# A routed feed-forward layer in row tiles of 128 instead of 256, two inner blocks per round, rows transposed two tiles ahead

## The chip, the core and the metric

The kernel is one program on one core of a Trainium2 chip. The metric is the device time of one execution, in microseconds (us); a measurement is the median of several executions. TensorE (PE) multiplies, and loads the stationary operand of a matmul by an instruction of its own (LDWEIGHTS, shown as PEld); VectorE (DVE) and ScalarE (ACT) work on elements, GpSimd (POOL) and SyncE (SP) here issue DMA transfers. Every engine runs its own instruction stream, in order. Streams are held together by semaphores: an engine raises one with an instruction (`then_inc`), another waits for it (`wait_ge`).

## The reference

A block of two attention layers and two routed feed-forward layers on 4 x 512 tokens of width 256, float32. The change touches the last layer alone. It has 8 experts in 4 groups of 2; each token goes to one group (the largest sigmoid score), and within it both experts are used with normalised weights:

```python
macro_scores = jax.nn.sigmoid(xf @ macro_w)
mv, mi = _topk_normalized(macro_scores, GROUPS_TOP_K)        # one group of four
micro_scores = jax.nn.sigmoid(jnp.einsum('td,gde->tge', xf, micro_w))
uv, ui = _topk_normalized(micro_scores, TOP_K)               # both experts of a group
...
gate = jax.nn.silu(jnp.einsum('td,edf->tef', xf, gate_w))    # inner width 512
up = jnp.einsum('td,edf->tef', xf, up_w)
h = gate * up
out = jnp.einsum('te,tef,efd->td', w, h, down_w)
```

The result is added to the residual stream.

## The kernel before

`build` runs seven phases one after the other; each ends with all engines done. The last two are `phase_route1` and `phase_experts1`. The first normalises the rows, picks each token's group, and scatters the rows (256 values, two weights and the token's number) into the scratch array `sorted`, ordered by group. Each group's rows begin at a multiple of TILE, so that every tile of TILE rows belongs to one group. With TILE = 256 there are 2048/256 + 3 = 11 tiles, 2816 rows with the padding; the table `tile_group` says which group a tile belongs to. All tiles are worked, padded rows too.

`phase_experts1` works tile by tile. Its weights, `experts1`, lie in SBUF as two half-precision parts, hi and lo, and so do the activations; each product is three matmuls (`three_products`, lines 197 to 199: hi by hi, lo with hi, hi with lo). Call such a group of three matmuls a triple. A tile has two parts in TensorE's program:

- `head`: four 128x128 transposes of the tile's rows into `h_tb` (line 1766); then the first layer, 8 blocks of the inner width (2 experts x 4) of 4 triples each (gate and up, two halves of the 256-wide input). The weights are the stationary operand, the turned rows the moving one, 256 columns wide. A block fills one of two `h_hb` buffers.
- `tail`: the second layer, for each half of 128 rows 8 triples into `h_ob`, with the inner activations stationary and 256 columns of `down` moving: 16 triples.

That is 96 + 48 matmuls a tile, all with 256 columns moving, and 1584 in all.

Around it, ACT copies the turned rows to half precision (`xt.hi`, line 1700) and DVE forms the rest (`xt.lo`, line 1720). For each block ACT applies silu (line 1705), DVE multiplies (`h`, line 1725), ACT and DVE split the product into `hs` (lines 1710, 1728). After the second layer DVE weighs and adds the two experts (`first`, `res`, lines 1734 and 1739), and POOL scatters the result with an accumulating indirect DMA (line 1691, one for each 128 rows), always after the scatters of the tile before have landed. SP loads tiles (line 1674).

`run_tiles` gives PE, ACT and DVE the same order: head 0, then head j+1 before tail j; two tiles make one turn of a loop (`Fori`). On PE the wait that a first layer begins with is for the `xt.lo` of its own tile, right behind its transposes (line 1768). A block waits until the `h_hb` that it overwrites has been read by DVE (line 1771).

Which group a tile has is known only at run time. `expert_base` (line 1753) therefore loads a register from `tile_group`, and every address in `experts1` is computed from it by register instructions in PE's own stream.

Of the kernel before, what the change touches and what calls it, by code (L numbers as in the profile page):

```python
# [8 lines left out]
ALU = mybir.AluOpType  # L9
ACT = mybir.ActivationFunctionType  # L10
# [6 lines left out]
P = 128  # L17
# [1618 lines left out]
def phase_experts1(nc, sem, T, dram, out):  # L1636

    with ExitStack() as ctx:
        sb, ps = make_tensors(nc, ctx)
        rows = [sb(f"h_rows{i}", [P, 2, ROW]) for i in range(2)]  # L1640
        weight = [sb(f"h_weight{i}", [P, 2, PER_GROUP + 1]) for i in range(2)]
        token = [sb(f"h_token{i}", [P, 2], I32) for i in range(2)]
        xt = [Split(sb, f"h_xt{i}", [P, DT, TILE]) for i in range(2)]
        silu = [sb(f"h_silu{i}", [P, TILE]) for i in range(2)]
        h = [sb(f"h_h{i}", [P, TILE]) for i in range(2)]
        HT = PER_GROUP * FT1
        hs = [Split(sb, f"h_hs{i}", [P, HT, TILE]) for i in range(2)]
        first = [sb(f"h_first{i}", [P, 2, D]) for i in range(2)]
        res = [sb(f"h_res{i}", [P, 2, D]) for i in range(2)]
        tb = [ps(f"h_tb{i}", [P, DT, TILE]) for i in range(2)]  # L1650
        hb = [ps(f"h_hb{i}", [P, 2, TILE]) for i in range(2)]
        ob = [[ps(f"h_ob{i}_{n}", [P, PER_GROUP, D]) for n in range(2)] for i in range(2)]
        names = ("rows_in0", "rows_in1", "turned", "xt_hi", "rows_free", "xt_lo", "h_full", "silu_ok", "h_ok", "h_hi", "h_lo", "out_done",
                 "first_ok", "res_ok", "res_free", "stored")
        (rows_in0, rows_in1, turned, xt_hi, rows_free, xt_lo, h_full, silu_ok, h_ok, h_hi, h_lo, out_done,
         first_ok, res_ok, res_free, stored) = (sem("h" + n) for n in names)
        rows_in = (rows_in0, rows_in1)

        def run_tiles(eng, head, tail):

            head(0, 0)
            with eng.Fori(0, TILES1 // 2) as m:
                head(m * 2 + 1, 1)
                tail(m * 2, 0)
                head(m * 2 + 2, 0)
                tail(m * 2 + 1, 1)
            tail(TILES1 - 1, 0)

        with nc.Block() as block:

            @block.sync
            def _(sp):
                def load(j):
                    sp.dma_start(rows[j % 2][:], dram["sorted"][j * TILE:(j + 1) * TILE, :].rearrange("(n p) d -> p n d", p=P)).then_inc(rows_in[j % 2], 16)

                load(0)
                load(1)
                for j in range(2, TILES1):
                    sp.wait_ge(rows_free, j - 1)
                    load(j)  # L1680

            @block.gpsimd
            def _(pool):
                pool.sem_inc(res_free, 2)
                for j in range(TILES1):
                    pool.wait_ge(res_ok, j + 3)
                    if j >= 1:
                        pool.wait_ge(stored, 32 * j)
                        pool.sem_inc(res_free, 1)
                    for n in range(2):  # L1690
                        pool.indirect_dma_start(out=out, out_offset=bass.IndirectOffsetOnAxis(ap=token[j % 2][:, n:n + 1], axis=0),  # L1691
                                                in_=res[j % 2][:, n, :], in_offset=None, bounds_check=B * S - 1, oob_is_err=False,
                                                compute_op=ALU.add).then_inc(stored, 16)
                pool.wait_ge(stored, 32 * TILES1)

            @block.scalar
            def _(act):
                def head(j, i):
                    act.wait_ge(turned, j + 1)
                    nc.scalar.activation(xt[i].hi[:], tb[i][:], ACT.Copy).then_inc(xt_hi, 1)  # L1700
                    for g in range(HT + 1):
                        if g < HT:
                            act.wait_ge(h_full, j * HT + (g + 1))
                            act.wait_ge(h_ok, j * HT + (g + 1))
                            nc.scalar.activation(silu[g % 2][:], hb[g % 2][:, 0, :], ACT.Silu).then_inc(silu_ok, 1)
                        if g >= 1:
                            act.wait_ge(h_ok, j * HT + (g + 2))
                            if g == 1:
                                act.wait_ge(out_done, j + 1)
                            nc.scalar.activation(hs[i].hi[:, g - 1, :], h[(g - 1) % 2][:], ACT.Copy).then_inc(h_hi, 1)  # L1710

                run_tiles(act, head, lambda j, i: None)

            @block.vector
            def _(dve):
                def head(j, i):
                    dve.wait_ge(xt_hi, j + 1)
                    dve.wait_ge(res_ok, j + 1)
                    nc.vector.tensor_copy(weight[i][:], rows[i][:, :, D:ROW]).then_inc(rows_free, 1)  # L1719
                    nc.vector.tensor_tensor(xt[i].lo[:], tb[i][:], xt[i].hi[:], ALU.subtract).then_inc(xt_lo, 1)  # L1720
                    for g in range(HT + 1):
                        if g < HT:
                            dve.wait_ge(silu_ok, j * HT + (g + 1))
                            dve.wait_ge(h_lo, j * HT + (g + 1))
                            nc.vector.tensor_tensor(h[g % 2][:], hb[g % 2][:, 1, :], silu[g % 2][:], ALU.mult).then_inc(h_ok, 1)
                        if g >= 1:
                            dve.wait_ge(h_hi, j * HT + g)
                            nc.vector.tensor_tensor(hs[i].lo[:, g - 1, :], h[(g - 1) % 2][:], hs[i].hi[:, g - 1, :], ALU.subtract).then_inc(h_lo, 1)

                def tail(j, i):  # L1730
                    dve.wait_ge(out_done, j + 3)
                    dve.wait_ge(res_ok, j + 1)
                    for n in range(2):
                        nc.vector.tensor_scalar(first[i][:, n, :], ob[i][n][:, 0, :], weight[i][:, n, 0:1], None, ALU.mult).then_inc(first_ok, 1)  # L1734
                    dve.wait_ge(first_ok, j * 2 + 2)
                    dve.wait_ge(res_free, j + 1)
                    nc.vector.tensor_copy(token[i][:], weight[i][:, :, PER_GROUP])  # L1737
                    for n in range(2):
                        op = nc.vector.scalar_tensor_tensor(out=res[i][:, n, :], in0=ob[i][n][:, 1, :], scalar=weight[i][:, n, 1:2],  # L1739
                                                            in1=first[i][:, n, :], op0=ALU.mult, op1=ALU.add)  # L1740
                    op.then_inc(res_ok, 1)
# [5 lines left out]
                run_tiles(dve, head, tail)  # L1747

            @block.tensor
            def _(pe):  # L1750
# [9 lines left out]
                def head(j, i):  # L1760
# [3 lines left out]
                    for n in range(2):  # L1764
                        for c in range(DT):
                            mm = pe.transpose(tb[i][:, c, n * P:(n + 1) * P], rows[i][:, n, c * P:(c + 1) * P], T.ident[:])
                    mm.then_inc(turned, 1)
                    pe.wait_ge(xt_lo, j + 3)
                    for g in range(HT):
                        expert, f = g // FT1, g % FT1  # L1770
                        pe.wait_ge(h_ok, j * HT + (g + 1))
                        for which, start in enumerate((GATE1, UP1)):
                            for c in range(DT):
                                mm = three_products(pe, hb[g % 2][:, which, :], weights(base, expert * EXPERT_COLS + start + c * FF1 + f * P, P),
                                                    (xt[i].hi[:, c, :], xt[i].lo[:, c, :]), c == 0, c == DT - 1)
                        mm.then_inc(h_full, 1)

                def tail(j, i):
                    base = expert_base(j)
                    pe.wait_ge(h_lo, j * HT + (HT + 2))  # L1780
                    pe.wait_ge(res_ok, j + 1)
                    for n in range(2):
# [8 lines left out]
                run_tiles(pe, head, tail)  # L1791

class Tensors:
# [85 lines left out]
```

## Time and profile before

| | |
|---|---|
| median of 3 executions | 1425.09 us (1423.35 to 1429.33) |
| span of the profiled execution, first to last instruction | 1427.3 us |
| PE busy, PEld busy | 1138.1 us (80%), 860.6 us (60%) |
| DVE, ACT, POOL busy | 798.9 us, 627.2 us, 507.8 us |
| granted TensorE clock, mean over the span | 0.901 |

The profile gives no time of its own for the profiled execution beside its span, and that span lies 2.2 us above the median and inside the range of the three. "Busy" for PE is not PE at its peak, since matmuls overlap in the pipeline: the start-to-start distance of matmuls says how fast they pass.
### The profile page before, as it was taken

What the parts mean: (1) busy time and instruction counts of PE and PEld (TensorE: products, weight loads), DVE (VectorE), ACT (ScalarE), POOL (GpSimd) and SP (SyncE); (2) the same over time, 40 slices, a digit from 0 to 9 for tenths busy, and PEclk for the clock granted to TensorE, in tenths of its full rate; (3) what the DMA queues carried; (4) which work ended last, traced back from release to release, by engine and by line L of the source; (5) the groups of instructions that cost most, each with busy time, mean ns of one, the idle gap of its engine ahead of it and who ended that gap; (6) DMA issues with size and microseconds to landing.
All of it is one profiled execution on the core that took longest, in us unless ns stands there. A gap on an engine that the chain in (4) does not pass through costs nothing. (4 is left out here: it accounts for less than half of the span.)

```text
span 1427.3 us, 30050 instructions
## 1 busy us (share of the span) xinstructions
PE 1138.1 (80%) x10895; PEld 860.6 (60%) x10896; DVE 798.9 (56%) x2325; ACT 627.2 (44%) x1171; POOL 507.8 (36%) x491
## 2 busy tenths in 40 slices
PE   2499999999999998338899455488999654988896
PEld 1166777777777776335788323355666343777775
DVE  7177887787688775758101163466777522444443
ACT  4177786787687774200222032144555312332231
POOL 2656454455544241300444230789300022011112
PEclk9899999999999999655899769799999856999999
DMA  6122223213212120700265415455311231111010
GB/s 235 52 60 63 66 57 78 55 46 79 65 46 67 47 50 20 238 28 2 96 185 170 110 42 186 124 161 158 91 47 39 73 95 62 19 27 28 19 15 8
DMA packets 80218, 110.88 MB, mean 78 GB/s; under 512 B 11552, under 2 KB 58400, under 8 KB 79712
## 3 DMA queue, kind: packets, MB, share of 16 engines
q1 hardware_dynamic: 69632, 88.23, 21.2%
q0 software_dynamic: 10464, 21.01, 6.4%
q8 instruction: 78, 1.28, 0.4%
q14 instruction: 44, 0.36, 0.1%
HBM read 59.86 MB, written 24.70 MB: 59 GB/s over the span
## 5 line engine op out<-in xcount | busy, mean ns | idle before, releaser
L542 DVE CUSTOM_DVE_ANT_0 masked<-sc,mask_bias 128x512 f32<-128x512 f32 x256 | 175.5, 686 | 58.0 <-issue 41.1
L518 DVE TENSOR_TENSOR e_t_lo<-et,e_t_hi 128x512 f16<-128x512 f32 x256 | 176.7, 690 | 50.9 <-ACT e_t_hi L484 48.5
L491 ACT ACTIVATE e<-masked,neg_max 128x512 f32<-128x512 f32 x256 | 184.1, 719 | 27.2 <-DVE neg_max L542 26.6
L484 ACT ACTIVATE e_t_hi<-et 128x512 f16<-128x512 f32 x256 | 152.0, 594 | 88.6 <-PE et L435 88.1
L435 PEld LDWEIGHTS et<-ident,e 128*128 128x128 f32 x1024 | 125.6, 141 | 54.1 <-ACT e L491 6.8
L435 PE MATMUL et<-ident,e 128*128 128x128 f32 x1024 | 154.1, 273 | 1.4 <-ACT e L491 0.7
L1266 ACT ACTIVATE d_e<-d_st 128x384 f32<-128x384 f32 (+1 forms) x192 | 98.0, 528 | 117.1 <-PE d_st L1351 101.1
L197 PE MATMUL h_hb<-h_xt_hi,experts_hi 128*128 128x256 f16 x352 | 101.5, 288 | 26.5 <-DVE h_xt_lo L1720 26.5
L197 PE MATMUL ob<-v_hi,e_t_hi 128*128 128x65 f16 x1024 | 119.0, 193 | 0.6 <-DVE e_t_lo L518 0.6
L198 PE MATMUL ob<-v_lo,e_t_hi 128*128 128x65 f16 x1024 | 119.2, 193 | 0.0
L199 PE MATMUL ob<-v_hi,e_t_lo 128*128 128x65 f16 x1024 | 118.4, 193 | 0.0
L1691 POOL DMA_INDIRECT out<-h_res,h_token x22 | 34.2, 1553 | 201.6 <-DVE h_res L1739 196.2
L427 PE MATMUL sc<-kk,qq 128*128 128x512 f16 x256 | 96.9, 379 | 6.5 <-DMA qq<-nat_q 6.3
L198 PE MATMUL h_hb<-h_xt_lo,experts_hi 128*128 128x256 f16 x352 | 101.4, 288 | 0.0
L199 PE MATMUL h_hb<-h_xt_hi,experts_lo 128*128 128x256 f16 x352 | 101.1, 287 | 0.0
L428 PE MATMUL sc<-kk,qq 128*128 128x512 f16 x256 | 96.9, 379 | 0.0
L198 PEld LDWEIGHTS ob<-v_lo,e_t_hi 128*128 128x128 f16 x1024 | 94.5, 97 | 2.9
L197 PEld LDWEIGHTS ob<-v_hi,e_t_hi 128*128 128x128 f16 x1024 | 95.7, 97 | 0.8 <-DVE e_t_lo L518 0.7
L199 PEld LDWEIGHTS ob<-v_hi,e_t_lo 128*128 128x128 f16 x1024 | 94.8, 97 | 0.0
L1346 PE MATMUL d_wk<-d_k,d_q 128*128 128x384 f16 (+1 forms) x256 | 72.5, 311 | 24.9 <-DMA d_q<-d_k 21.2
L478 ACT ACTIVATE raw<-pj 128x512 f32<-128x512 f32 x128 | 75.0, 586 | 33.2 <-POOL v_lo L335 14.7
L1278 DVE TENSOR_REDUCE d_mx<-d_wk 128x1 f32<-128x384 f32 x128 | 66.9, 553 | 37.5 <-PE d_wk L1351 31.7
(315 smaller groups left out, 2906.6 us busy)
## 6 DMA issues: line engine op xcount, KB each, us to landing
kk<-nat_k SPq DMA_DIRECT2D x128, 128.0 KB, 2.3
raw<-in_fc SPq DMA_DIRECT2D x16, 1024.0 KB
qq<-nat_q SPq DMA_DIRECT2D x128, 64.0 KB, 2.0
mask_raw<-in_mask SPq DMA_DIRECT2D x16, 256.0 KB, 2.8
scratch_stack<-c_qk_hi SPq DMA_DIRECT2D x32, 128.0 KB
scratch_stack<-c_qk_lo SPq DMA_DIRECT2D x32, 128.0 KB
d_expert_raw<-in_gate_w POOLq DMA_DIRECT2D x8, 512.0 KB, 4.4
d_expert_raw<-in_up_w POOLq DMA_DIRECT2D x8, 512.0 KB, 4.0
```

Of the source, the lines that this page charges most:

```text
L197: pe.matmul(out, stat[0], mov[0], start=first, stop=False)
L198: pe.matmul(out, stat[0], mov[1], start=False, stop=False)
L199: return pe.matmul(out, stat[1], mov[0], start=False, stop=last)
L427: pe.matmul(sc[j % 2][:], stat, kk[g % 2][:, a, 0, :], start=True, stop=False)
L428: pe.matmul(sc[j % 2][:], stat, kk[g % 2][:, a, 1, :], start=False, stop=True).then_inc(scores, 1)
L435: mm = pe.transpose(et[u % 2][:, kt, :], e[u % NBUF][:, kt * P:(kt + 1) * P], T.ident[:])
L478: nc.scalar.activation(raw[n % NRAW][:], pj[GROUP0[what] % 2][:], ACT.Copy).then_inc(copied, 1)
L484: nc.scalar.activation(e_t[u % NBUF].hi[:], et[u % 2][:], ACT.Copy).then_inc(turned_hi, 1)
L491: nc.scalar.activation(e[u % NBUF][:], masked[u % NBUF][:], ACT.Exp, bias=neg_max[:, g % 2, j:j + 1], scale=-1.0).then_inc(exp_ok, 1)
L518: nc.vector.tensor_tensor(e_t[u % NBUF].lo[:], et[u % 2][:], e_t[u % NBUF].hi[:], ALU.subtract).then_inc(turned_lo, 1)
L542: nc.vector.tensor_tensor_reduce(masked[u % NBUF][:], sc[j % 2][:], mask_bias[g // PAIRS % 2][:, j % QT, :], -SCALE0, 3e38, ALU.add, ALU.m ...
L1266: nc.scalar.activation(part(e[m % EBUF][:, 2 * half + i // 3, :, :], i % 3), src, ACT.Exp, scale=SCALE1).then_inc(exp_ok, 1)
```

## The change

TILE becomes 128, so there are 2048/128 + 3 = 19 tiles, 2432 rows with the padding. In the first layer the moving operand is now 128 columns wide. A round takes two blocks of the inner width together, so that silu, `h` and the two splits keep their size of 128 x 256 elements, and a tile has 4 rounds of 8 triples. The second layer of a tile has 8 triples instead of 16, with 256 columns moving as before; 2 transposes a tile instead of 4; and one scatter instead of two. A tile's `head` is taken apart into `turn` (transposes, `xt.hi`, `xt.lo`) and the first layer, and the turn of tile j+2 now stands between the first layer of tile j+1 and the tail of tile j, on PE, ACT and DVE alike. In `phase_route1` the tables follow TILE.

```diff
-TILE = 2 * P
+TILE = P
...
-        def run_tiles(eng, head, tail):
-
-            head(0, 0)
-            with eng.Fori(0, TILES1 // 2) as m:
-                head(m * 2 + 1, 1)
-                tail(m * 2, 0)
-                head(m * 2 + 2, 0)
-                tail(m * 2 + 1, 1)
-            tail(TILES1 - 1, 0)
+        def run_tiles(eng, turn, first, tail):
+
+            turn(0, 0)
+            first(0, 0)
+            turn(1, 1)
+            with eng.Fori(0, TILES1 // 2 - 1) as m:
+                first(m * 2 + 1, 1)
+                turn(m * 2 + 2, 0)
+                tail(m * 2, 0)
+                first(m * 2 + 2, 0)
+                turn(m * 2 + 3, 1)
+                tail(m * 2 + 1, 1)
+            first(TILES1 - 2, 1)
+            turn(TILES1 - 1, 0)
+            tail(TILES1 - 3, 0)
+            first(TILES1 - 1, 0)
+            tail(TILES1 - 2, 1)
             tail(TILES1 - 1, 0)
...
-                def head(j, i):
-                    base = expert_base(j)
+                def turn(j, i):
                     pe.wait_ge(xt_lo, j + 1)
                     pe.wait_ge(rows_in[i], (j - i) * 8 + 16)
-                    for n in range(2):
-                        for c in range(DT):
-                            mm = pe.transpose(tb[i][:, c, n * P:(n + 1) * P], rows[i][:, n, c * P:(c + 1) * P], T.ident[:])
+                    for c in range(DT):
+                        mm = pe.transpose(turned_bank(i)[:, c, :], rows[i][:, c * P:(c + 1) * P], T.ident[:])
                     mm.then_inc(turned, 1)
+
+                def first_layer(j, i):
+                    base = expert_base(j)
                     pe.wait_ge(xt_lo, j + 3)
-                    for g in range(HT):
-                        expert, f = g // FT1, g % FT1
-                        pe.wait_ge(h_ok, j * HT + (g + 1))
+                    for g in range(GR):
+                        pe.wait_ge(h_ok, j * GR + (g + 1))
                         for which, start in enumerate((GATE1, UP1)):
-                            for c in range(DT):
-                                mm = three_products(pe, hb[g % 2][:, which, :], weights(base, expert * EXPERT_COLS + start + c * FF1 + f * P, P),
-                                                    (xt[i].hi[:, c, :], xt[i].lo[:, c, :]), c == 0, c == DT - 1)
+                            for n in range(2):
+                                expert, f = (2 * g + n) // FT1, (2 * g + n) % FT1
+                                for c in range(DT):
+                                    mm = three_products(pe, hb[g % 2][:, which, n, :], weights(base, expert * EXPERT_COLS + start + c * FF1 + f * P, P),
+                                                        (xt[i].hi[:, c, :], xt[i].lo[:, c, :]), c == 0, c == DT - 1)
                         mm.then_inc(h_full, 1)
...
-                    for n in range(2):
-                        for expert in range(PER_GROUP):
-                            for f in range(FT1):
-                                g = expert * FT1 + f
-                                mm = three_products(pe, ob[i][n][:, expert, :], (hs[i].hi[:, g, n * P:(n + 1) * P], hs[i].lo[:, g, n * P:(n + 1) * P]),
-                                                    weights(base, expert * EXPERT_COLS + DOWN1 + f * D, D), f == 0, f == FT1 - 1)
+                    for expert in range(PER_GROUP):
+                        for f in range(FT1):
+                            g = expert * FT1 + f
+                            mm = three_products(pe, ob[i][:, expert, :], (hs[i].hi[:, g, :], hs[i].lo[:, g, :]),
+                                                weights(base, expert * EXPERT_COLS + DOWN1 + f * D, D), f == 0, f == FT1 - 1)
```

ACT and DVE are taken apart in the same way; on DVE the copy of the weights moves from ahead of `xt.lo` to the start of the first layer.

How the change moves instructions is seen best on PE. The first place is the end of a first layer in the loop (that of tile 2m+1) and what follows it.
```order
L197 ISA
L197 MATMUL h_hb1<-h_xt1_hi,experts1_hi 128x256
L198 MATMUL h_hb1<-h_xt1_lo,experts1_hi 128x256
L199 REGISTER_ALU
L199 MATMUL h_hb1<-h_xt1_hi,experts1_lo 128x256
L1753 ISA
L1753 TENSOR_LOAD tile_group
L1753 ISA x2
L1780 REGISTER_ALU
L197 ISA
L197 MATMUL h_ob0_0<-experts1_hi,h_hs0_hi 128x256
```

And in the changed kernel:

```order
L197 ISA
L197 MATMUL h_hb1<-h_xt1_hi,experts1_hi 128x128
L198 MATMUL h_hb1<-h_xt1_lo,experts1_hi 128x128
L199 REGISTER_ALU
L199 MATMUL h_hb1<-h_xt1_hi,experts1_lo 128x128
L1778 REGISTER_ALU
L1779 ISA
L1781 MATMUL h_tb0<-ident,h_rows0 128x128 x2
L1770 ISA
L1770 TENSOR_LOAD tile_group
L1770 ISA x2
L1799 REGISTER_ALU
```

The triple keeps its two register instructions while its matmuls are half as wide, and the transposes now stand ahead of the tail. The second place is the end of that tail. Before, its second half of rows is multiplied without register instructions, and the transposes come between it and the next first layer:

```order
L197 MATMUL h_ob0_1<-experts1_hi,h_hs0_hi 128x256
L198 MATMUL h_ob0_1<-experts1_lo,h_hs0_hi 128x256
L199 MATMUL h_ob0_1<-experts1_hi,h_hs0_lo 128x256
L1753 ISA
L1753 TENSOR_LOAD tile_group
L1753 ISA x2
L1762 REGISTER_ALU
L1763 ISA
L1766 MATMUL h_tb0<-ident,h_rows0 128x128 x4
L1768 REGISTER_ALU
L1771 REGISTER_ALU
L197 ISA
```

In the changed kernel:

```order
L197 ISA
L197 MATMUL h_ob0<-experts1_hi,h_hs0_hi 128x256
L198 REGISTER_ALU
L198 MATMUL h_ob0<-experts1_lo,h_hs0_hi 128x256
L199 MATMUL h_ob0<-experts1_hi,h_hs0_lo 128x256
L1770 ISA
L1770 TENSOR_LOAD tile_group
L1770 ISA x2
L1786 REGISTER_ALU
L1788 REGISTER_ALU
L197 ISA
L197 MATMUL h_hb0<-h_xt0_hi,experts1_hi 128x128
```

There every triple has its register instructions, and nothing but the table's load and waits stands between the tail and the next first layer.

## Rows read from the trace of the kernel before

**Rows 1.** Busy time in stretches: start:end, us, engines, PEclk, DMA share, GB/s.
```profile
core 0: us, PE busy (x) PEld busy (x) DVE busy (x) ACT busy (x) POOL busy (x), PEclk, DMA share, GB/s
1196.90:1417.50 220.60, 192.47 (x1624) 163.72 (x1624) 93.56 (x246) 68.15 (x187) 30.14 (x20) 0.95 0.13 21
1252.45:1271.83 19.38, 16.50 (x149) 14.41 (x149) 8.74 (x23) 6.22 (x17) 3.09 (x3) 1.00 0.17 27
1271.83:1292.77 20.94, 18.16 (x148) 15.25 (x149) 8.73 (x23) 6.22 (x17) 3.09 (x3) 0.92 0.12 20
1272.29:1275.70 3.41, 3.41 (x19) 2.43 (x17) 0.42 (x1) 0.38 (x1) 2.40 (x2) 0.50 0.58 106
855.90:886.60 30.70, 15.53 (x73) 6.08 (x72) 8.80 (x13) 7.56 (x11) 0.00 (x0) 1.00 0.54 185
```

**Rows 2.** One group from 1190 us on: busy, mean ns | idle before, releaser.
```profile
L197 PE MATMUL h_hb<-h_xt_hi,experts_hi 128*128 128x256 f16 x352 | 101.5, 288 | 26.5 <-DVE h_xt_lo L1720 26.5
```

**Rows 3.** In order of time, from the end of one tile's second layer.
```profile
1268.66 0.60 PE L1766 MATMUL h_tb<-ident,h_rows 128*128 128x128 f32 x4
...
1269.30 0.60 ACT L1700 ACTIVATE h_xt_hi<-h_tb 128x512 f16<-128x512 f32 x1 [4.87 <-PE h_tb L1766]
...
1270.90 0.68 DVE L1720 TENSOR_TENSOR h_xt_lo<-h_tb,h_xt_hi 128x512 f16<-128x512 f32 x1
...
1271.83 0.28 PE L197 MATMUL h_hb<-h_xt_hi,experts_hi 128*128 128x256 f16 x1 [2.56 <-DVE h_xt_lo L1720]
```

**Rows 4.** In order of time, the last two blocks of a first layer.
```profile
1282.56 0.27 PE L199 MATMUL h_hb<-h_xt_hi,experts_lo 128*128 128x256 f16 x1
...
1282.87 0.38 ACT L1705 ACTIVATE h_silu<-h_hb 128x256 f32<-128x256 f32 x1 [0.62 <-PE h_hb L199]
...
1283.29 0.42 DVE L1725 TENSOR_TENSOR h_h<-h_hb,h_silu 128x256 f32<-128x256 f32 x1 [0.55 <-ACT h_silu L1705]
...
1283.87 0.27 PE L199 MATMUL h_hb<-h_xt_hi,experts_lo 128*128 128x256 f16 x1
...
1284.35 0.10 PEld L197 LDWEIGHTS h_ob<-experts_hi,h_hs_hi 128*128 128x128 f16 x1 [0.49 <-issue]
```

**Rows 5.** TensorE's sequencer, line 197, in 1282.43:1283.17 and 1284.1:1289.5.
```profile
L197 PEldq FUSED_REGOPS  x4: 46/46/46, 1282.4 to 1283.2; - x4
...
L197 PEldq FUSED_REGOPS  x8: 46/46/60, 1284.2 to 1285.9; - x8
```

**Rows 6.** Sequencer, line 1753 in 1283.3:1284.3; lines 1662, 1753 in 1247.0:1248.2.
```profile
L1753 PEldq TENSOR_LOAD <-tile_group x1: 298/298/298, 1283.4 to 1283.4; - x1
...
L1662 PEldq ALU_OP  x1: 32/32/32, 1247.3 to 1247.3; - x1
...
L1753 PEldq TENSOR_LOAD <-tile_group x1: 302/302/302, 1247.8 to 1247.8; - x1
```

**Rows 7.** In order of time, second attention layer.
```profile
960.22 0.22 PE L1349 MATMUL d_wk<-band,ident 128*128 128x128 bf16 x1
960.27 0.22 PE L1351 MATMUL d_wk<-band,ident 128*128 128x128 bf16 x1
```

**Rows 8.** In order of time, start of the stage.
```profile
1194.26 1.08 PE L1766 MATMUL h_tb<-ident,h_rows 128*128 128x128 f32 x4 [30.27 <-DMA h_rows<-scratch_sorted]
...
1196.92 0.39 PE L197 MATMUL h_hb<-h_xt_hi,experts_hi 128*128 128x256 f16 x1 [1.58 <-DVE h_xt_lo L1720]
```

**Rows 9.** In order of time, end of the kernel.
```profile
1416.87 1.55 POOL L1691 DMA_INDIRECT out<-h_res,h_token  x1 [0.30 <-issue]
...
1417.21 0.27 PE L199 MATMUL h_ob<-experts_hi,h_hs_lo 128*128 x1
...
1418.51 0.87 DVE L1739 SCALAR_TENSOR_TENSOR h_res<-h_ob,h_weight,h_first 128x256 f32<-128x256 f32 x2
...
1420.45 1.55 POOL L1691 DMA_INDIRECT out<-h_res,h_token  x1 [2.02 <-DMA out<-h_res,h_token]
...
1422.30 1.55 POOL L1691 DMA_INDIRECT out<-h_res,h_token  x1 [0.30 <-issue]
```

More of the change, by code:

```diff
@@ L1694, in _ @@
-                pool.wait_ge(stored, 32 * TILES1)
+                    pool.indirect_dma_start(out=out, out_offset=bass.IndirectOffsetOnAxis(ap=token[j % 2][:, 0:1], axis=0),
+                                            in_=res[j % 2][:], in_offset=None, bounds_check=B * S - 1, oob_is_err=False,
+                                            compute_op=ALU.add).then_inc(stored, 16)
+                pool.wait_ge(stored, 16 * TILES1)
             @block.scalar
             def _(act):
-                def head(j, i):
+                def turn(j, i):
@@ L1699, in head @@
                     act.wait_ge(turned, j + 1)
[L1700 to L1705, printed above, removed]
+                    nc.scalar.activation(xt[i].hi[:], turned_bank(i), ACT.Copy).then_inc(xt_hi, 1)
@@ L1706, in head @@
+                def first_layer(j, i):
+                    for g in range(GR + 1):
+                        if g < GR:
+                            act.wait_ge(h_full, j * GR + (g + 1))
+                            act.wait_ge(h_ok, j * GR + (g + 1))
+                            nc.scalar.activation(silu[g % 2][:], hb[g % 2][:, 0, :, :], ACT.Silu).then_inc(silu_ok, 1)
                         if g >= 1:
-                            act.wait_ge(h_ok, j * HT + (g + 2))
+                            act.wait_ge(h_ok, j * GR + (g + 2))
@@ L1717, in head, with first_layer @@
                     dve.wait_ge(xt_hi, j + 1)
+                    nc.vector.tensor_tensor(xt[i].lo[:], turned_bank(i), xt[i].hi[:], ALU.subtract).then_inc(xt_lo, 1)
+                def first_layer(j, i):
                     dve.wait_ge(res_ok, j + 1)
[L1719 to L1725, printed above, removed]
+                    nc.vector.tensor_copy(weight[i][:], rows[i][:, D:ROW]).then_inc(rows_free, 1)
+                    for g in range(GR + 1):
+                        if g < GR:
+                            dve.wait_ge(silu_ok, j * GR + (g + 1))
+                            dve.wait_ge(h_lo, j * GR + (g + 1))
+                            nc.vector.tensor_tensor(h[g % 2][:], hb[g % 2][:, 1, :, :], silu[g % 2][:], ALU.mult).then_inc(h_ok, 1)
@@ L1732, in tail @@
                     dve.wait_ge(res_ok, j + 1)
-                    for n in range(2):
-                        nc.vector.tensor_scalar(first[i][:, n, :], ob[i][n][:, 0, :], weight[i][:, n, 0:1], None, ALU.mult).then_inc(first_ok, 1)
-                    dve.wait_ge(first_ok, j * 2 + 2)
+                    nc.vector.tensor_scalar(first[i][:], ob[i][:, 0, :], weight[i][:, 0:1], None, ALU.mult).then_inc(first_ok, 1)
+                    dve.wait_ge(first_ok, j + 1)
                     dve.wait_ge(res_free, j + 1)
[L1737 to L1741, printed above, removed]
+                    nc.vector.tensor_copy(token[i][:], weight[i][:, PER_GROUP:PER_GROUP + 1])
+                    nc.vector.scalar_tensor_tensor(out=res[i][:], in0=ob[i][:, 1, :], scalar=weight[i][:, 1:2],
+                                                   in1=first[i][:], op0=ALU.mult, op1=ALU.add).then_inc(res_ok, 1)
                 dve.sem_inc(xt_lo, 2)
@@ L1746, in _ @@
                 dve.sem_inc(res_ok, 2)
-                run_tiles(dve, head, tail)
+                run_tiles(dve, turn, first_layer, tail)
             @block.tensor
```

52 lines of the change are left out of this document (27 added, 25 removed).

## The prediction

> **What bounds the kernel now.** I read the windows first. From the first matmul of the stage to its last there are 220.3 us [rows 8, 9], in which TensorE is busy for 192.5 at a mean granted clock of 0.95 [rows 1]. DVE (93.6), ACT (68.2), POOL (30.1) and the DMA engines (0.13) are far from full. So the stage is TensorE's. The groups by line then say what its idle time waits for: 26.5 us stand before the first matmul of a first layer, all of it released by `xt.lo` [rows 2]. The timeline of one tile shows this wait: transposes at 1268.66, `xt.hi` at 1269.30, `xt.lo` at 1270.90, first matmul at 1271.83 [rows 3], so 3.17 us with nothing but the turn between second and first layer. After it the clock is at 0.50 (1.2 GHz) for 3.41 us in most tiles [rows 1]; the tile that begins so lasts 20.94 us and the one at 1.00 lasts 19.38.
>
> Next, the pace. Matmul 1282.56 to matmul 1283.87 are 12 in 1.31 us [rows 4], 0.109 each with 256 columns, 0.327 for a triple. The reader should now look below the matmuls, at the sequencer, which runs ahead of the array where it can. Line 197's register instruction opens a triple; its starts are four in 1282.4 to 1283.2 (exactly, 0.72 us, the edges of the view) and eight in 1284.2 to 1285.9 [rows 5], that is 0.24 us for a triple, while the array takes 0.327. Today this pace is hidden behind the array. That is what the change meets.
>
> **First layer.** Triples a tile stay 32, matmuls a tile 96, each with 128 columns. For the array, the nearest rows are 128-column matmuls with fixed addresses, 0.05 to 0.055 apart [rows 7], so 0.16 a triple. The sequencer still has two register instructions, three loads and three matmuls in every triple, none of which depends on the width, and needs 0.238 (the two rows of [rows 5] give 0.24 and 0.243 rounded; finer reading of their edges gives 0.237 to 0.24). The longer one decides: 32 x 0.238 = 7.62 us. Three of the four round waits cost the sequencer some 0.09 each, an estimate from two register instructions of 46 ns [rows 5]: 0.27. Together 7.89 for 128 rows; before, 10.5 for 256. The total number of first-layer triples goes from 352 to 608, and they get cheaper by only a quarter.
>
> **Turn and second layer.** The turn costs the sequencer two waits and two transposes, 0.17 (an estimate; below it 0.1, above it half of the 0.60 of [rows 3]). The tail begins with the table's load: from the load at 1283.4 to the first register instruction of the tail at 1284.2 [rows 5, 6] are 0.84, with what stands before it 0.88. Before, this lay half behind the array, which had work queued until 1283.87 and resumed at 1284.35 [rows 4]; now the sequencer is the later one and every bit counts. Eight triples then take the sequencer 8 x 0.238 = 1.90, the array 24 x 0.109 = 2.62; meanwhile the sequencer is already in the next first layer's load and waits (0.90, the same rows), and arrives after 2.80. So the array's 2.62 are hidden, and the tile pays 1.90 + 0.90.
>
> **Sum of a tile:** 7.89 + 0.17 + 0.88 + 1.90 + 0.90 = 11.74; times 19 = 223.1. The loop's edge sets the load at 1247.8 after a register instruction at 1247.3 [rows 6], some 0.39 more than without an edge, eight times: 3.1. The first tile's load is done while the stage waits for its rows (-0.9), the last tail is the array's (+0.6), and the first 3.4 us run at 0.50, where a triple of 128 columns takes 0.32 instead of 0.238 (+0.9). That makes 226.8 against 220.3: **+6.5**. The removed gap (11 x 3.17 = 35 us) and the lost cold stretches are all in this comparison: what they give is eaten because nearly twice as many tiles (19 for 11) each pay 7.9 us of sequencer for a first layer whose array work is 5.3, and two loads of the table in the open.
>
> **Around it.** At the start, before the first matmul: two transposes fewer in 1.08 for four [rows 8] plus shorter copies. `xt.hi` of 256 elements a row goes from 0.60 to about 0.41 and `xt.lo` from 0.68 to 0.42, by silu's 0.38 and `h`'s 0.42 for that size [rows 3, 4]; the copy of the weights is out of the way. That gives -1.0, and half the bytes of the first load perhaps -0.3 (0 to -1.4). At the end, the scatters chain: 1416.87 to 1420.45 across tiles, 1420.45 to 1422.30 within one, then 5.0 to the end of the span [rows 9]. Before, the last stands 5.09 after the last matmul at 1417.21. Now a tile has one; the second-last begins some 0.9 before the last matmul, the last 3.58 after it, at +2.69, and `res` is ready by then (1418.51 + 0.87, with two halves, is +2.17 already). So -2.4. The routing's table has more entries: +0.1. **Net +2.9.** The profiled span of 1427.3 is 2.2 above the median of the runs; I add the difference to the median, 1425.1, and get **1428**.
>
> **What I cost at nothing, and its cover.** The turned rows: last matmul of a round to the end of `h` is 1.15 us [rows 4]; behind it ACT does the split (0.41) and `xt.hi` (0.41), DVE `xt.lo` (0.42), 2.4 us in all, and TensorE's sequencer needs 0.88 + 1.90 + 0.90 = 3.7 before it wants them. If the cover were gone, each us over 3.7 costs 19. A round's buffer: chain of 1.15 plus start-up 0.16 against a round of 8 x 0.238 = 1.90. One scatter in 11.7 us against 3.58. SP loads a tile one whole tile ahead. The new waits on PE (lines 1778, 1779) hold up the tail behind them, hence the splits and DVE's `first`, but what they wait for (`xt.lo` of the tile before, rows long loaded) is done.
>
> **The rivals.**
> *A, forecast:* the sequencer sets the pace. Bounds: 0.23 to 0.245 a triple over 760 triples is -6 to +5 us, load and waits 0.1 either way in each tile is 2 us. Own range 1420 to 1436. **Chance 0.74.**
>
> *B, the array or the load of weights sets the pace*, and register instructions cost nothing where the queue is deep: 96 x 0.055 + 24 x 0.109 + 0.5 for what the load leaves open (0.48 in [rows 4]) = 8.4 a tile, 160 in 19, plus 0.9: 59 less than now, with start and end **1362**. Against it stands [rows 5]: nothing shows a triple of the sequencer below 0.237. **0.05.** The Trainium skill ("TensorE: Matmul & The Clock Gate", "Back-to-back issue gap") gives two figures for 128 columns: some 56 ns for the isolated gap, which is B, and some 81 ns sustained for pairs of load and matmul. By the second the first layer is 96 x 0.081 = 7.8 us, nearly my 7.89, but with another cause: the time would stay at about 1426 with fixed addresses too. [rows 7] speak against that for a short piece (0.055); no row here shows a long one.
>
> *C, the other side: the clock falls in every tile although no long gap is left.* TensorE's array is now busy for 5.3 of 7.9 us in the first layer. If 3.4 us a tile (as after today's gaps, [rows 1]) run at 0.50, a 128-column triple takes 0.32 instead of 0.238, 0.88 a tile, in 18 tiles +16: **1444**. It decides from the point where the clock falls without a gap like today's 2.56 [rows 3]. For it: the array works in a thinner stream than ever in this stage. Against it: from 855.9 to 886.6 PE was busy for 15.5 of 30.7 us, less than here, and kept 1.00 [rows 1]; the longest gap here is 1.1 (turn and load). If the whole stage stayed at 0.50, the tail would be the array's as well (24 x 0.213 = 5.1 for 2.8) and the sum about 1520. **0.13**, 0.02 of it for the whole stage. The Trainium skill (same page, "Why this matters for your kernels") speaks against the change here: with thin row blocks the clock goes to and fro, 25.9% of peak at M = 128. No row here shows that in a stage with 128-column matmuls in sequence.
>
> *D, a chain that I have hidden is not* (the turned rows over 3.7 us, a buffer late each round), or the load is better hidden than I think: 1400 to 1460, both sides alike. **0.08.**
>
> **How the numbers follow.** Half a per cent, 7.1 us, is about what a measurement of this kernel can tell from none. Under 1418: B, a third of D, a tail of A (0.04): 0.12. Over 1432.2: C, a third of D, 0.06 of A: 0.22. Between: 0.66. The range goes from 1415 to 1445: A, C's middle and half of D, a little over 8 in 10; B and the cold stage are left out.
>
> **What would show it.** First-layer matmuls in sets of three, a set every 0.238, TensorE's idle time released by "issue" and not by `xt.lo`; from one tile's first matmul to the next 11.7 us; 608 triples. Right for the turn: no idle time behind L1720. Wrong if a round starts on `h_ok` (then a buffer), if sets are 0.16 apart (B), if PEclk of a stretch in mid-stage is 0.50 (C), or if tiles are 11.7 but the end comes otherwise (start and end terms).

## The result

| | before | after |
|---|---|---|
| median | 1424.2 us (1419.69 to 1429.33, 4 runs) | 1436.8 us (1435.45 to 1439.19, 4 runs) |
| span of the profiled execution | 1427.3 us | 1435.1 us |
| mean granted clock | 0.901 | 0.909 |

The ratio to before is 1.0091, 95% interval 1.0066 to 1.0116: the kernel is slower by 0.9%. That lies in the range that was forecast (1415 to 1445), but outside the half per cent of the likeliest case, above 1432.2, which had 0.22. It also lies just above the 1420 to 1436 that rival A, whose mechanism the traces show, had as its own range.

In stretches of the changed kernel (start:end, us, busy time and instructions of each engine, granted clock, DMA share, GB/s):

```profile
core 0: us, PE busy (x) PEld busy (x) DVE busy (x) ACT busy (x) POOL busy (x), PEclk, DMA share, GB/s
1193.40:1426.30 232.90, 214.72 (x2316) 162.92 (x2316) 86.88 (x242) 60.21 (x171) 27.19 (x18) 0.99 0.11 19
1253.70:1278.16 24.46, 22.62 (x244) 16.93 (x244) 9.30 (x27) 6.28 (x18) 3.10 (x2) 1.00 0.13 22
...
1203.41:1206.83 3.42, 2.88 (x28) 2.88 (x29) 0.38 (x2) 0.10 (x1) 0.00 (x0) 0.50 0.14 39
```

This answers to [rows 1]. From the first matmul of a first layer to the last of the kernel there are now 232.6 us (1193.43 to 1426.00), against 220.3. TensorE's granted clock is 1.00 where it was 0.95: besides the stage's first 3 us only one stretch of 3.42 us at 0.50 is left. And two tiles last 24.46 us, 12.23 each. So nearly everything that the turn cost is gone, the clock is up, there are 14% fewer rows, and the stage is 12 us longer. The groups say the same (busy, mean ns | idle before, releaser), to be read beside [rows 2]:

```profile
L197 PE MATMUL h_hb<-h_xt_hi,experts_hi 128*128 128x128 f16 x608 | 139.1, 230 | 7.8 <-issue 3.9 <-DVE h_xt_lo L1735 3.1
...
L197 PE MATMUL h_ob<-experts_hi,h_hs_hi 128*128 x152 | 41.6, 274 | 11.3 <-issue 11.3
```

The 26.5 us behind `xt.lo` have become 3.1, and no wait for another engine has come in their place (what is left is released by "issue"). "PE busy" hides the rest, because a 128-column matmul of 0.22 us overlaps the next even when that starts 0.08 later. The loss only shows on the sequencer. Its register instructions in one first layer, the load of the table behind it and ahead of the next, the eight triples of the tail between them, and the two loads of the tile after (one source line each; first and last start):

```profile
L197 PEldq FUSED_REGOPS  x32: 46/46/46, 1253.6 to 1261.4; - x32
...
L1770 PEldq TENSOR_LOAD <-tile_group x2: 301/306/311, 1262.0 to 1264.9; - x2
...
L197 PEldq FUSED_REGOPS  x8: 46/46/60, 1262.9 to 1264.6; - x8
...
L1770 PEldq TENSOR_LOAD <-tile_group x2: 299/300/300, 1273.9 to 1277.2; - x2
```

32 triples start from 1253.6 to 1261.4, 0.25 apart on average with the waits of the rounds; read to the nanosecond, a triple is 0.1130 + 0.1240 = 0.237 us, as forecast. [rows 5] had 0.24 for the same two instructions, at twice the width.

### The profile page after: what moved, and what is told of

It is laid out like the page before. It is cut to its first block and busy times, and to the rows that moved or that the text cites. A ratio compares the mean times of both kernels' runs of the same rounds, so it can differ in the third digit from the quotient of the medians.

```text
span 1435.1 us, 32119 instructions
## 1 busy us (share of the span) xinstructions
PE 1158.1 (81%) x11585; PEld 859.0 (60%) x11586; DVE 791.2 (55%) x2319; ACT 619.0 (43%) x1155; POOL 503.1 (35%) x488
## 3 DMA queue, kind: packets, MB, share of 16 engines
q1 hardware_dynamic: 68992, 87.44, 20.5%
## 5 line engine op out<-in xcount | busy, mean ns | idle before, releaser
L491 ACT ACTIVATE e<-masked,neg_max 128x512 f32<-128x512 f32 x256 | 184.4, 720 | 27.0 <-DVE neg_max L542 26.5
L197 PE MATMUL h_hb<-h_xt_hi,experts_hi 128*128 128x128 f16 x608 | 139.1, 230 | 7.8 <-issue 3.9
L198 PE MATMUL h_hb<-h_xt_lo,experts_hi 128*128 128x128 f16 x608 | 134.2, 222 | 0.0
L199 PE MATMUL h_hb<-h_xt_hi,experts_lo 128*128 128x128 f16 x608 | 133.9, 221 | 0.0
L1706 POOL DMA_INDIRECT out<-h_res,h_token x19 | 29.5, 1554 | 216.0 <-DVE h_res L1757 213.0
L1722 ACT ACTIVATE h_silu<-h_hb 128x256 f32<-128x256 f32 x76 | 29.2, 384 | 164.2 <-PE h_hb L199 164.2
L1744 DVE TENSOR_TENSOR h_h<-h_hb,h_silu 128x256 f32<-128x256 f32 x76 | 32.3, 425 | 109.7 <-ACT h_silu L1722 109.7
```

The costliest lines, as they stand in the source:

```text
L197: pe.matmul(out, stat[0], mov[0], start=first, stop=False)
L198: pe.matmul(out, stat[0], mov[1], start=False, stop=False)
L199: return pe.matmul(out, stat[1], mov[0], start=False, stop=last)
L491: nc.scalar.activation(e[u % NBUF][:], masked[u % NBUF][:], ACT.Exp, bias=neg_max[:, g % 2, j:j + 1], scale=-1.0).then_inc(exp_ok, 1)
```

## The experiments

Each median stands beside runs of before on the same chip. static_after, lo_static, ahead256 and not_ahead ran on one chip, the two with reuse and the two with extra_reg on another, so rows of different sets are better compared by their ratios. "Stage" is from the first transpose to the end of the profiled span, "first layer" from its first matmul to its last, in mid-stage.

| kernel | median | ratio to before (95%) | stage | first layer | a tile |
|---|---|---|---|---|---|
| before | 1424 to 1426 | 1 | 233.0 | 10.4, 12.0 with a stretch at 0.50 | 20.5 |
| after | 1436.8 | 1.0091 (1.0066 to 1.0116) | 243.3 | 7.93 | 12.2 |
| static_after | 1362.8 | 0.954 (0.9504 to 0.9575) | 172.2 | 5.30 | 8.2 |
| lo_static | 1372.0 | 0.961 (0.9574 to 0.9644) | 178.0 | 5.30 | 8.6 |
| ahead256 | 1387.6 | 0.973 (0.9675 to 0.978) | 198.4 | 10.6 | 16.6 |
| not_ahead | 1456.8 | 1.021 (1.0168 to 1.0244) | 264.5 | 7.91 | 13.4 |
| reuse | 1430.1 | 1.0035 (1.0008 to 1.0061) | 237.9 | 7.93 | 11.9 |
| ahead256_reuse | 1392.2 | 0.976 (0.9719 to 0.9802) | 197.2 | 10.6 | 16.5 |
| extra_reg | 1512.6 | 1.060 (1.0564 to 1.0634) | 321.5 | 12.0 | 16.3 |
| extra_reg256 | 1408.3 | 0.988 (0.9827 to 0.9927) | 219.3 | 12.0 | 18.5 |

**static_after: no registers in TensorE's stream**

```diff
                 def expert_base(j):
-                    group = pe.value_load(T.tile_group[0:1, bass.ds(j, 1)], min_val=0, max_val=GROUPS1 - 1)
-                    return group * (PER_GROUP * EXPERT_COLS)
+                    return 0
```

> Changed kernel, but TensorE always takes group 0's weights at fixed addresses, so no register instruction and no load of the table is left in its stream; matmuls, waits and sizes are the same (the values are those of group 0 for every tile). Theory 1 (two register instructions a triple hold the sequencer at 0.237 us): the array takes over, a set of three 128-column matmuls passes in 0.163, a tile in 8.1 to 8.6 us, the kernel 1355 to 1375. Theory 2 (a pair of load and matmul with 128 columns cannot pass faster than some 0.079, whatever the registers do): first layer stays at 7.6 us or more, only the loads of the table fall away, 10.3 us a tile, about 1399.

Measured 1362.8, 74 less than the changed kernel with the same matmuls. A first layer, by the first of its 32 triples and the last:

```profile
L197 PE MATMUL h_hb<-h_xt_hi,experts_hi x32: 219/219/219, 1231.1 to 1236.3; 128*128 128x128 f16 x32
```

5.2 us for 31 triples, 0.168 within the 0.1 to which the row rounds. Rival B had 1362 for the array alone. That the two agree to a microsecond is in part chance: B's tile of 8.4 us held 0.5 for the load of the table, which this run leaves out, and the tile measured 8.2. Theory 2, a floor for pairs of load and matmul, has fallen: in a first layer of 96 the pairs pass 0.056 apart. (By the Trainium skill, "TensorE: Matmul & The Clock Gate", section "Back-to-back issue gap", 128 columns sustain some 81 ns a matmul; these rows have 56 for 96 in a row, which is its figure for the isolated gap. What gave 0.079 in the changed kernel was the registers.)

**lo_static: one register instruction a triple instead of two**

```diff
-                    cols = bass.ds(base + col, n)
-                    return T.experts1.hi[:, cols], T.experts1.lo[:, cols]
+                    return T.experts1.hi[:, bass.ds(base + col, n)], T.experts1.lo[:, bass.ds(col, n)]
```

> Changed kernel, only the lo part of the weights at a fixed address (group 0's lo part), so one register instruction a triple instead of two; the loads of the table stay. Theory 1: spacings of the changed kernel's sequencer (0.124 from the fused instruction to the next, 0.113 from that one back) with about 0.09 for a lone register instruction leave 0.144 to 0.15 a triple, so the array's 0.163 decides: tile about 9.1 us, kernel 1370 to 1390. If a register instruction cost only its own 0.032 us: 0.205 a triple, about 1412. Theory 2: first layer unchanged, within 5 us of 1437.

Measured 1372.0. The sequencer, line 197, in 1253.05:1253.50, and then the matmuls of a first layer:

```profile
L197 PEldq FUSED_REGOPS  x4: 46/46/46, 1253.1 to 1253.5; - x4
```

```profile
L197 PE MATMUL h_hb<-h_xt_hi,experts_hi x32: 219/219/219, 1217.6 to 1222.8; 128*128 128x128 f16 x32
```

Four register instructions in 0.4 us (0.124 apart to the nanosecond): the sequencer now is the faster one (the expectation had 0.144 to 0.15 for it), and the first layer is the array's, 5.30, the same as with no register at all. What is left between this and static_after, 0.4 us a tile, is the load of the table: a tile takes 8.6 us, where the expectation had 9.1.

**extra_reg, extra_reg256: one register instruction more in each triple of the first layer**

```diff
+                def three_addresses(pe, out, base, col, mov, first, last):
+                    hi, lo = weights(base, col, P)
+                    other = weights(base, col + P // 2, P)[0]
+                    pe.matmul(out, hi, mov[0], start=first, stop=False)
+                    pe.matmul(out, other, mov[1], start=False, stop=False)
+                    return pe.matmul(out, lo, mov[0], start=False, stop=last)
...
-                                    mm = three_products(pe, hb[g % 2][:, which, n, :], weights(base, expert * EXPERT_COLS + start + c * FF1 + f * P, P),
+                                    mm = three_addresses(pe, hb[g % 2][:, which, n, :], base, expert * EXPERT_COLS + start + c * FF1 + f * P,
...
```

> Changed kernel with one register instruction more in each triple of the first layer: the second matmul takes its stationary block at another address computed at run time (64 columns on, so its product is not the reference's). Theory 1: from the spacings, 0.084 us for a fused register instruction, so a triple takes 0.32 instead of 0.237, 608 x 0.084 = 51 us: 1483 to 1493. Theory 2 (pair of load and matmul is the floor and the register instructions hide below it): no change, 1437.

> The same extra register instruction in 256-row tiles turned ahead, 352 triples. Theory 1: the sequencer's 0.32 us a triple is still under the array's 0.327, so only the sequencer's lead goes and the loads of the table come into the open, up to 1.5 us a tile: 1388 to 1404, against the 30 us that 352 x 0.084 would be where the sequencer binds.

Measured 1512.6 and 1408.3: both costs were put too low. With 128 columns the stage is 78.2 us longer, 0.129 for each of the 608 added instructions (0.128 by the first layer in mid-stage), not 0.084. I had split the spacing wrongly: a register instruction with the matmuls behind it takes 0.113 to 0.124, and those matmuls add next to nothing, so the third costs as much as each of the first two: most triples of extra_reg are 0.124 + 0.124 + 0.113 = 0.361 us. The two kernels side by side are the clearest rows of this study; first 128 columns, the sequencer's instructions and the matmuls:

```profile
L1780 PEldq FUSED_REGOPS  x32: 46/46/46, 1239.9 to 1251.6; - x32
...
L1780 PE MATMUL h_hb<-h_xt_hi,experts_hi x32: 227/227/228, 1240.0 to 1251.7; 128*128 128x128 f16 x32
```

and with 256 columns:

```profile
L1779 PE MATMUL h_hb<-h_xt_hi,experts_hi x32: 272/280/282, 1247.1 to 1258.8; 128*128 128x256 f16 x32
```

11.7 us from the first triple to the last in both, 0.377 a triple. At three register instructions a triple the width of a matmul no longer matters in the first layer: 256 columns cost what 128 do. Against its own base (ahead256) the 256-column kernel pays 20.9 us of stage for the same instruction, because there the array's 0.327 had covered two of the three.

So over the dose of 0, 1, 2 and 3 register instructions a triple, the first layer of 128 columns takes 5.30, 5.30, 7.93 and 12.0 us; 256 columns take 10.6 with 2 and 12.0 with 3.

**ahead256: only the turn is moved, the tiles stay at 256 rows**

```diff
-                def head(j, i):
-                    base = expert_base(j)
+                def turn(j, i):
...
+                def first_layer(j, i):
+                    base = expert_base(j)
                     pe.wait_ge(xt_lo, j + 3)
```

`run_tiles` is that of the changed kernel, and ACT and DVE are taken apart in the same way.

> Kernel before (256-row tiles, one block a round), with nothing changed but that the turn of tile j+2 stands between the first layer of j+1 and the tail of j. Theory 1 (width is what loses, turning ahead is what gains): a triple stays the array's at 0.327, the gap of 2.84 us before ten first layers goes, the clock stays up: 16.9 us a tile, kernel 1388 to 1400. If the clock still falls in most tiles (1.6 us each): about 1407. Rival (turning ahead gives nothing, since another wait ends just then): 1420 to 1428.

Measured 1387.6, 37 less than before: the best kernel here that computes the reference. That is the lower edge of what was expected (1388 to 1400); a tile takes 16.6 us, not 16.9. Two tiles, then the stage from first matmul to last (windows), and the wait (groups):

```profile
1239.51:1272.66 33.15, 32.90 (x298) 28.78 (x296) 17.66 (x46) 12.20 (x34) 6.17 (x4) 1.00 0.18 29
1190.79:1376.60 185.81, 182.37 (x1624) 159.03 (x1624) 94.20 (x246) 67.05 (x187) 29.87 (x20) 0.99 0.15 25
```

```profile
L197 PE MATMUL h_hb<-h_xt_hi,experts_hi 128*128 128x256 f16 x352 | 97.1, 276 | 4.3 <-DVE h_xt_lo L1732 3.9
```

Of the 26.5 us that [rows 2] puts down to `xt.lo`, 3.9 are left. Of the stretches at 0.50, which made six of the first layers of before 1.4 to 1.7 us longer, none is left: from 1195.46 to the last matmul the clock is 1.00.

**not_ahead: only the tiles are halved, each is turned right ahead of its own first layer**

```diff
             turn(0, 0)
             first(0, 0)
-            turn(1, 1)
-            with eng.Fori(0, TILES1 // 2 - 1) as m:
+            with eng.Fori(0, TILES1 // 2) as m:
+                turn(m * 2 + 1, 1)
                 first(m * 2 + 1, 1)
-                turn(m * 2 + 2, 0)
                 tail(m * 2, 0)
+                turn(m * 2 + 2, 0)
                 first(m * 2 + 2, 0)
-                turn(m * 2 + 3, 1)
                 tail(m * 2 + 1, 1)
...
```

> Changed kernel with the turn of a tile put back right ahead of its own first layer, so 128-row tiles alone. Theory 1: some 2.4 us of gap (DVE does first and res of the tile before ahead of xt.lo) in place of a load of the table behind the array: +1.7 us a tile, and the clock falls after it in most tiles, up to +0.9: 1465 to 1485. Rival (the turn in the open costs little, because the sequencer has its 0.93 us to do there anyway): 1440 to 1450.

Measured 1456.8, between what the theory and its rival gave. The turn in order of time:

```profile
1238.52 0.38 PE L1775 MATMUL h_tb<-ident,h_rows 128*128 128x128 f32 x2
...
1239.31 0.47 DVE L1751 SCALAR_TENSOR_TENSOR h_res<-h_ob,h_weight,h_first 128x256 f32<-128x256 f32 x1
1239.70 0.41 DVE L1729 TENSOR_TENSOR h_xt_lo<-h_tb,h_xt_hi 128x256 f16<-128x256 f32 x1
...
1240.35 0.10 PEld L197 LDWEIGHTS h_hb<-h_xt_hi,experts_hi 128*128 x1 [1.69 <-issue]
```

`xt.lo` does stand behind `res` on DVE, but the way from transposes to first matmul is 1.83 us, and between the layers there are 1.94, where I had expected 2.4. And the clock fell in only two tiles, not in most. So turning ahead is worth some 20 us at 128 rows (a tile 13.4 to 12.2), and 37 at 256.

**reuse, ahead256_reuse: one load of the table fewer in every second tile**

```diff
                 def first_layer(j, i):
-                    base = expert_base(j)
+                    base = kept[i] = expert_base(j)
...
                 def tail(j, i):
-                    base = expert_base(j)
+                    base = kept[1] if i == 1 else expert_base(j)
```

> Changed kernel, but the tail of every second tile takes the base register that its own first layer loaded, so nine of the 38 loads of the table go. Theory 1 (the sequencer is the bound, so that its load and register instructions count in full, 0.80 to 0.83 us each): 7 us less, 1428 to 1431. Rival (the load lies behind the array's queue, as half of it did before): 0 to 3 us less.

> 256-row tiles turned ahead, with the same reuse of the base register in five of eleven tails. Theory 1: here the array is the bound and stands idle 0.17 to 0.41 us between first layer and tail instead of the 0.11 between any two matmuls; at most 0.3 us in five places: 0 to 1.5 us less than turning ahead alone, that is 1386 to 1388, not to be told from it.

Measured 1430.1 (ten runs, 1423.5 to 1437.3) for the first, inside 1428 to 1431; the stage is 5.4 us shorter, 0.6 for each of nine loads, where 0.80 to 0.83 was expected. The second has 1392.2, above the 1386 to 1388 expected, but its interval overlaps that of ahead256, and the stage is 1.3 us shorter, inside the expected 0 to 1.5. The same edit is worth 5 us where the sequencer is the bound and about 1 where the array is.

## Why the prediction was right, and where it was off

**The bound.** "The longer one decides", the sequencer's 0.238 against the array's 0.163: right. The triple measured 0.237. Taking one of the two register instructions away, or both, gives the array's 5.30 us, and adding one lengthens the layer at both widths to the same 12.0. This is shown, not argued. What stays open is why a register instruction costs some 0.12 us while its own row says 46 ns or 32: whether the sequencer or the load that depends on the address waits was not separated. In the changed kernel that load starts 0.095 us after the start of the fused instruction, and 0.060 after that of the other.

**The turn is hidden.** Right. In the changed kernel, the turn of one tile and the first matmul of the next first layer:

```profile
1261.87 0.44 PE L1781 MATMUL h_tb<-ident,h_rows 128*128 128x128 f32 x2
...
1263.12 0.37 ACT L1715 ACTIVATE h_xt_hi<-h_tb 128x256 f16<-128x256 f32 x1
...
1263.59 0.42 DVE L1735 TENSOR_TENSOR h_xt_lo<-h_tb,h_xt_hi 128x256 f16<-128x256 f32 x1
...
1265.87 0.23 PE L197 MATMUL h_hb<-h_xt_hi,experts_hi 128*128 128x128 f16 x1
```

`xt.lo` ends at 1264.0, 2.1 us after the transposes; that tile's first layer is a whole tile away, and even the next begins only at 1265.87. No round waited on `h_ok`.

**The clock** (rival C): did not come in the changed kernel, whose loop runs at 1.00 from 1206.83 on, 2.9 us into its first tile. But the clock can fall without a long gap. In extra_reg, where the same matmuls are spread over 12.0 us instead of 7.9, the clock fell twice in mid-loop. The tile ahead, and the two falls (windows):

```profile
1239.95:1253.28 13.33, 12.67 (x98) 9.20 (x99) 3.28 (x10) 2.63 (x8) 1.59 (x1) 1.00 0.12 20
1253.49:1256.89 3.40, 3.40 (x18) 2.41 (x17) 0.76 (x2) 0.30 (x2) 0.00 (x0) 0.50 0.00 0
1308.10:1311.50 3.40, 3.40 (x28) 2.59 (x27) 0.42 (x1) 0.41 (x2) 0.20 (x1) 0.50 0.09 8
```

The first begins 0.2 us into a tail, with no idle time of TensorE's array over 1 us ahead of it in that tile, and the second 2.9 us into a first layer. So a gap like that of [rows 3] is not the condition that I took it for. That the thinner stream caused these two is likely but not shown: they are two tiles of nineteen in one profile. (The Trainium skill, "TensorE: Matmul & The Clock Gate", "Why this matters for your kernels", has the clock go to and fro with thin row blocks unless all blocks of the contracted dimension are worked before the next transfer, or the rows are padded. This kernel works them in a row, so that sentence was no argument against it, and in the changed kernel's loop the clock stayed at 1.00 after that first stretch.)

The price that C had for a fall, 0.88 us a tile, was wrong too. The tail in which the clock fell lasts 4.19 us from first to last matmul instead of 2.52, but the first layer behind it takes 10.64 instead of 12.02, so that the two tiles from 1239.95 to 1272.62 last 32.67 us, against 32.65 for the undisturbed pair from 1321.47 to 1354.12. The first layer with the second fall takes 12.03, no more than the others. Where the sequencer is the bound, it goes on at its pace while the array falls behind, and the array catches up afterwards. The start of the changed kernel's stage shows both parts: the stretch at 0.50 (windows), then line 197 in 1193.43:1196.59 and in 1196.61:1197.6.

```profile
1193.43:1196.59 3.16, 3.16 (x30) 3.12 (x31) 0.00 (x0) 1.08 (x2) 0.00 (x0) 0.50 0.16 42
```

```profile
L197 PEldq FUSED_REGOPS  x12: 46/46/46, 1193.6 to 1196.3; - x12
...
L197 PE MATMUL h_hb<-h_xt_hi,experts_hi x6: 219/219/220, 1196.6 to 1197.4; 128*128 128x128 f16 x6
```

Twelve triples pass the sequencer at 0.50, 0.24 apart as at 1.00, while the array starts 30 matmuls, 0.107 apart; from 1196.6 on its triples pass 0.17 apart until it has caught up. A stretch at 0.50 of this length costs the stage next to nothing where the sequencer decides, and some 1.6 us where the array does, as in before.

**The sum of a tile**, forecast 11.74 and 0.2 for the loop's edge, was mis-sized by 0.3, which is 5 us of the 5.8 by which the stage from matmul to matmul was missed (forecast 226.8, measured 232.6). The first layer takes the sequencer 8.06 (1253.6 to 1261.4 and one triple), not 7.89: in the loop about one triple in seven takes 0.03 more than the others, and one in nine 0.01 more, for which I have no cause. Turn and load take 1.20 in one tile and 1.01 in the other, forecast 1.05; the tail 1.96, forecast 1.90; the next load 0.93 and, at the loop's edge, 1.32, forecast 0.90 and 1.29. The first layer is the largest part, and of the rest all but one are off the same way by a few hundredths up to 0.15; there are 19 tiles. Besides, the first two tiles of the loop last 12.55 and 12.75, 0.4 more than those after them; no run shows why.

**The second tile** was left out of the sum. The prologue has `turn(1)` directly ahead of `first(1)`, with no tail between, so that its turn is not covered:

```profile
1189.52 0.81 SPq L1690 DMA_DIRECT2D h_rows<-scratch_sorted  x2
...
1191.74 0.66 PE L1781 MATMUL h_tb<-ident,h_rows 128*128 128x128 f32 x2 [29.83 <-DMA h_rows<-scratch_sorted]
...
1193.43 0.28 PE L197 MATMUL h_hb<-h_xt_hi,experts_hi 128*128 128x128 f16 x1 [1.02 <-DVE h_xt_lo L1735]
...
1201.50 0.41 PE L1781 MATMUL h_tb<-ident,h_rows 128*128 128x128 f32 x2
...
1203.30 0.42 DVE L1735 TENSOR_TENSOR h_xt_lo<-h_tb,h_xt_hi 128x256 f16<-128x256 f32 x1
...
1203.95 0.28 PE L197 MATMUL h_hb<-h_xt_hi,experts_hi 128*128 128x128 f16 x1 [2.04 <-DVE h_xt_lo L1735]
```

From the transposes to the first matmul 2.45 us, some 1.4 more than the 0.17 and 0.90 that I had put there (the stretch at 0.50 from 1203.41 lies around its end). Part of it is made up by the first tile, for which the sum had +0.9 because of the clock at 0.50: its 96 matmuls take 7.95 us, the 7.93 of mid-stage within 0.02, since the array catches up as shown above.

**The start.** Transposes to first matmul: 1.69 against 2.66 of [rows 8], forecast -1.0, measured -0.97. From the load's issue at 1189.52 to the transposes 2.22, against 2.84 before, where the issue stands at 1191.42: -0.6 for half the bytes, forecast -0.3 with bounds to -1.4.

**The end.** Forecast -2.4, measured -1.0: the term rested on the wrong row. In order of time:

```profile
1425.54 1.55 POOL L1706 DMA_INDIRECT out<-h_res,h_token  x1 [10.15 <-DVE h_res L1757]
...
1426.00 0.27 PE L199 MATMUL h_ob<-experts_hi,h_hs_lo 128*128 x1
...
1426.90 0.48 DVE L1757 SCALAR_TENSOR_TENSOR h_res<-h_ob,h_weight,h_first 128x256 f32<-128x256 f32 x1
1430.13 1.55 POOL L1706 DMA_INDIRECT out<-h_res,h_token  x1 [3.04 <-DMA out<-h_res,h_token]
```

From one scatter's start to the next across tiles I took 3.58 [rows 9]. But that one was the second of a pair. A scatter by itself takes 4.59 until the next may start, and nearly the same in static_after and lo_static (4.57 and 4.61). The last one starts 4.1 after the last matmul, not 2.69.

**The sum in the end.** Net forecast +2.9; the medians say +12.6, the two profiled spans +7.8. Of the spans' difference, +12.3 is the stage from matmul to matmul, -1.0 the end, -3.5 the start; and 1.9 of that last is only that the phases ahead, whose work is the same, ended earlier in this execution. Without it +9.7, against the +2.9 of the forecast: 5.8 of the miss are in the stage from matmul to matmul (5.2 in the loop's sixteen tiles, 0.7 in the first and second tile together), 1.4 the end, less 0.3 at the start. The remaining 2.9 us up to the medians' 12.6 are not attributed: the profiled executions are single ones. So the mechanism was right and the change in time was put at less than a quarter of what came. That 1436.8 lies inside 1415 to 1445 is in part luck: the upper part of the range was there for C and D, and neither came.

## What to carry to other kernels

Where a stationary or moving operand's address is computed at run time, count register instructions in the engine's stream as a second bound beside the array's columns, and compare the two before an operand is made narrower: here 0.12 us for each, so that two a triple are nearly free at 256 columns and make the first layer half as long again at 128 (7.93 against 5.30). A change that bundles two edits can hide a good one: moving the turn alone gave 37 us, and halving the tiles took 49 back. Look at the sequencer's own rows; the busy share of TensorE rose in the stage while it did less work.

## What was unexpected of the hardware

- A register instruction in TensorE's stream that computes an address costs 0.113 to 0.128 us of its stream's pace, some three times its own row of 0.03 to 0.05, and three of them a triple make matmuls of 128 and 256 columns pass at the same 0.377 a triple.
- 96 loads and matmuls of 128 columns with fixed addresses pass in 5.30 us, 0.056 each, with a new stationary operand every time.
- The granted clock fell to 0.50 after six of the nine gaps of some 2.84 us in the kernel before, after two of the seventeen of some 1.7 us in not_ahead, and in extra_reg twice without a gap over 1 us. At the second tile it fell with gaps of 2.31 (after, static_after), 2.26 (reuse), 2.28 (extra_reg) and 2.57 us (extra_reg256), and not with 2.40 (lo_static) and 2.62 (ahead256, ahead256_reuse). The length of the gap alone does not say whether it falls.
- Where the sequencer was the bound, a stretch of 3.4 us at 0.50 cost next to nothing; where the array was, some 1.6 us.
- A scatter by itself frees the next after 4.6 us, the second of a pair after 3.58 from its own start.
- The first transpose of the stage starts anywhere from 1187.2 to 1194.3 us in ten profiled executions whose programs do the same work up to there, but for the routing's tables and the size of the first load. A difference of some us between two profiled spans should be read from stage to stage.
